# A two-layer convolution kernel: the first statistics read from row sums, two reductions for the kernel's sum, and other orders later

## The chip, the cores and the metric

The kernel runs on one core of a Trainium2 chip. The metric is the time of one execution on the device in microseconds, as the median of several runs. The engines are TensorE (PE in the profile, PEld its weight loads), VectorE (DVE), ScalarE (ACT), GpSimd (POOL) and SyncE (SP, which issues the DMAs). Each executes its own queue in order; semaphores tie them together.

## The reference

```python
# x: (16, 32, 48, 48) float32; L0 weight: (32, 32, 3), L0 bias: (32,); L1 weight: (32, 32, 5, 5)
def _L0_conv_ref(x, weight, bias):          # 9 x 9 Gaussian kernels made of (sx, sy, angle)
    w = _gaussian_kernels(weight, 9)        # exp(-q / 2), divided by its sum over the 81 taps
    out = conv(x, w, padding=4)
    return out + bias[None, :, None, None]
def _L1_conv_ref(x, weight):                # 5 x 5 convolution with reflected edges
...
def _gn(v, G=16, eps=1e-05):                # normalise each image's 16 groups of two channels
    g = v.reshape(B, G, C // G, H, W)
    return ((g - mean(g)) / sqrt(var(g) + eps)).reshape(v.shape)
x = x + _L0_conv_ref(_gn(x), L0_conv_weight, L0_conv_bias)
x = x + _L1_conv_ref(_gn(x), L1_conv_weight)
```

## The kernel before

The 16 images lie as 8 pairs in the on-chip array X, with channel and row modulo 4 on the 128 partitions. Two pairs are a quad (`qd`, four images), so layer 1 runs in four quads; layer 2 runs by pairs. Both convolutions are done along the rows with a short-filter transform: layer 1 makes 8 streams of 384 columns out of the normalised rows (`s32_1`), each is split into a 16-bit high half (`hi`, a copy by ScalarE) and a low half (`lo`, a subtraction by VectorE), and TensorE multiplies high by high, low by high and high by low weights (`whl`), nine taps each, 27 products per stream (`conv1`, `layer1`). The products of the streams are combined by ScalarE (`read_m1`: `mb`) and VectorE (`middle1`: `ps`, `pd`; `rows1`, `end1`) and added to X. Layer 2 does the same with four streams (`streams2`, `conv2`, `middle2`, `rows2`, `end2`).

There is no scheduler: each engine's order is written out by hand, VectorE's in `first_quad` to `last_steps`, ScalarE's and TensorE's at the end of their blocks. A helper's first argument is the layer or the quad. `low_halves(1, 2, range(2))` makes the first two low halves of layer 1's quad 2; `channel_sums(c, qd, images)` sums images and their squares on ScalarE, two passes for each image; `stats(c, qd)` is the product on TensorE that adds those sums over a group; `small_stats` turns them into scale (`gsc`) and offset (`gof`) on VectorE, with ScalarE's square root (`std`) in the middle.

The first quad is special, since the weights are made while it begins. VectorE makes the exponents of the Gaussian taps (`arg`), ScalarE the exponentials in two parts (3 taps, then 2), VectorE adds the blocks for stream 1 (`outer_blocks`, `all_blocks`, each in two parts), sums the kernel's taps (`tap_pairs`, `kernel_sum`) and multiplies by the reciprocal. Taps beyond the centre are made once and turned: through TensorE for streams 1 and 2 (`turn_partitions`, `turned_kernel`), by DMA for the rest (`turn_kernel`). `FIRST_PARTS` is TensorE's order of made and turned parts. Streams 1 and 2 of quad 0 don't wait for normalised images: TensorE sums raw rows (`near_rows`), and scale and offset are applied to the sums (`first_stream1`, `first_stream2`), so stream 1 needs X, the scale and the offset. The images' mean comes from `plain`: twelve products of X with the group matrix, 192 columns each, summed once more by `first_means` on VectorE. `warming` keeps TensorE at work until X lands.

## Time and profile before

| | |
|---|---|
| median of 3 runs | 241.84 us (240.73, 241.84, 244.12) |
| profiled execution | 240.74 us, span 238.9 us |
| busy: TensorE, VectorE, ScalarE | 97%, 89%, 66% of the span |
| the chain that ended last | PE 52%, DVE 34%, ACT 6%, issue 5% |

The span is from the first to the last instruction of the profiled execution; 1.8 us of its time lie around it. A matmul in 32-bit floats appears as two records. The chain is followed back from the last instruction, at each step to what released it; from 110.9 us on it is TensorE alone, before that mostly VectorE.

### The profile page before, as it was taken

The numbers are of one execution on the slowest core, as the hardware profiler recorded it, in microseconds if no ns is written. First come the engines' busy times: TensorE is split into PE (matmuls) and PEld (weight loads), VectorE is DVE, ScalarE is ACT, GpSimd is POOL, SyncE is SP. The second block draws the span as 40 slices with busy tenths as digits, with TensorE's granted clock in tenths as the row PEclk, the third lists the DMA queues.
The fourth block names the chain that finished last, engine by engine and source line by source line (L and its number), as shares of the span: only waits on it lengthen the run. The fifth ranks groups of instructions, "written<-read, shape, count | busy, mean of one in ns | idle before, by whom it ended". The sixth has DMA issues, their size and how long they took to land.

```text
span 238.9 us, 4161 instructions
## 1 busy us (share of the span) xinstructions
PE 231.8 (97%) x1445; PEld 144.2 (60%) x1445; DVE 211.5 (89%) x460; ACT 157.9 (66%) x329; POOL 4.5 (2%) x12
## 2 busy tenths in 40 slices
PE   6999999899999999999999999999999999999995
PEld 6855656555665665555666665556666665555554
DVE  5999999899999899999989998999997459978943
ACT  6979899897598487999637693537459004569310
POOL 1000000320000000000000000000000000000000
PEclk9999999999999999999999999999999999999999
DMA  7980122210034000003502000162020002521123
GB/s 211 377 344 4 36 54 68 67 44 0 3 103 112 3 1 0 3 0 105 186 26 99 0 4 0 35 171 111 1 101 0 0 0 59 155 102 60 44 99 99
DMA packets 8709, 17.24 MB, mean 72 GB/s; under 512 B 3312, under 2 KB 5616, under 8 KB 8688
## 3 DMA queue, kind: packets, MB, share of 16 engines
q1 hardware_dynamic: 7712, 16.64, 21.2%
q10 hardware_dynamic: 976, 0.34, 0.6%
q8 instruction: 11, 0.18, 0.3%
q14 instruction: 10, 0.08, 0.1%
HBM read 5.57 MB, written 4.72 MB: 43 GB/s over the span
## 4 chain that ended last, share of the span: by engine, by line
PE 52%; DVE 34%; ACT 6%; issue 5%; DMA 1%; DVEq 0%; ACTq 0%
PE banks L1477 28%; PE banks L1494 25%; DVE X L796 7%; DVE lo L763 4%; DVE whl L565 2%; ACT junk L1098 2%; DVE wl L590 1%; ACT hi L1154 1%; DVE work L560 1%; ACT P L1131 1%; DMA prm<-in_w 1%; DVE partU L712 1%; ACT arg L1178 1%; DVE s L496 1%; DVE partU L677 1%
## 5 line engine op out<-in xcount | busy, mean ns | idle before, releaser
L1477 PE MATMUL banks<-hi,whl 128*128 128x360 f16 (+4 forms) x576 | 98.2, 318 | 1.0 <-DVE pd L787 0.7
L1477 PEld LDWEIGHTS banks<-hi,whl 128*128 128x128 f16 x576 | 55.5, 98 | 35.4 <-DVE pd L787 1.0
L1477 PE MATMUL banks<-lo,whl 128*128 128x376 f16 (+4 forms) x288 | 51.2, 318 | 1.0 <-DVE lo L763 1.0
L1098 ACT ACTIVATE junk<-X 128x576 bf16<-128x576 f32 x56 | 41.1, 734 | 2.1 <-DVE X L796 0.5
L1477 PEld LDWEIGHTS banks<-lo,whl 128*128 128x128 f16 x288 | 27.8, 97 | 18.3 <-DVE lo L763 1.7
L1494 PE MATMUL banks<-lo,wh 128*128 128x384 f16 (+1 forms) x165 | 31.5, 320 | 0.0
L1494 PE MATMUL banks<-hi,wl 128*128 128x384 f16 (+1 forms) x165 | 31.5, 320 | 0.0
L1494 PE MATMUL banks<-hi,wh 128*128 128x384 f16 (+1 forms) x165 | 31.5, 320 | 0.0
L1154 ACT CAST hi<-work 128x416 f16<-128x416 f32 x32 | 16.6, 537 | 17.7 <-PE banks L1494 12.6
L1144 ACT ACTIVATE work<-work,gof,gsc 128x26 f32<-128x26 f32 (+1 forms) x48 | 24.9, 609 | 3.6 <-DVE gof L661 3.6
L1154 ACT CAST hi<-s 128x384 f16<-128x384 f32 x32 | 15.3, 510 | 16.6 <-DVE s L730 11.0
L1494 PEld LDWEIGHTS banks<-hi,wl 128*128 128x128 f16 x165 | 15.7, 96 | 10.5
L1494 PEld LDWEIGHTS banks<-lo,wh 128*128 128x128 f16 x165 | 15.7, 96 | 10.5
L1494 PEld LDWEIGHTS banks<-hi,wh 128*128 128x128 f16 x165 | 15.8, 96 | 10.4
L763 DVE TENSOR_TENSOR lo<-work,hi 128x416 f16<-128x416 f32 x32 | 17.4, 583 | 1.0 <-ACT hi L1154 0.8
L796 DVE SCALAR_TENSOR_TENSOR X<-pd,X 128x384 f32<-128x384 f32 x36 | 18.1, 558 | 0.0
L796 DVE SCALAR_TENSOR_TENSOR X<-ps,X 128x384 f32<-128x384 f32 x36 | 18.1, 558 | 0.0
L1131 ACT ACTIVATE P<-X,gof,gsc 128x336 f32<-128x336 f32 x28 | 17.2, 687 | 0.5 <-DVE gof L661 0.5
L763 DVE TENSOR_TENSOR lo<-s,hi 128x384 f16<-128x384 f32 x32 | 16.4, 552 | 0.6 <-ACT hi L1154 0.2
L786 DVE SCALAR_TENSOR_TENSOR ps<-banks,mb 128x384 f32<-128x384 f32 x12 | 6.6, 554 | 8.0 <-PE banks L1477 7.2
L1165 ACT ACTIVATE mb<-banks,bias 128x384 f32<-128x384 f32 x12 | 6.8, 568 | 7.7 <-PE banks L1477 7.7
L1098 ACT ACTIVATION_READ_ACCUMULATOR junk<-X 128x1 f32 x56 | 10.6, 190 | 0.0
(137 smaller groups left out, 232.0 us busy)
## 6 DMA issues: line engine op xcount, KB each, us to landing
X<-in_x SPq DMA_DIRECT2D x8, 576.0 KB, 9.4
out<-X SPq DMA_DIRECT2D x7, 576.0 KB, 2.8
work<-X SPq DMA_DIRECT2D x8, 432.0 KB, 3.8
whl<-work SPq DMA_DIRECT2D x24, 64.0 KB, 2.0
work<-X SPq DMA_DIRECT2D x8, 144.0 KB, 3.6
stage<-in_w SPq DMA_DIRECT2D x1, 640.0 KB, 7.3
work<-X SPq DMA_DIRECT2D x32, 12.0 KB, 2.3
out<-X SPq DMA_DIRECT2D x1, 384.0 KB, 2.6
```

Of the source, the lines that this page charges most:

```text
L496: done(tt(ca[:, at, :].rearrange("p k (e o) -> p k e o", o=C), centre.unsqueeze(1).to_broadcast([P, n, NE, C]), ak[:, at, :].unsqueeze(2). ...
L565: tt(made_taps(wl, i), weight1(i), made_taps(wh, i), ALU.subtract).then_inc(wl1_done, 1)
L763: tt(lo[c][:, i, :], src, hi[c][:, i, :], ALU.subtract).then_inc(lo_done[c], 1)
L786: stt(ps[1][:, :], product1(qd, k), f, mb[1][:, :], ALU.mult, ALU.add).then_inc(mid_done[1], 1)
L796: stt(out1(qd, k), tiled1(src[1][:, :]), factors[g][i], out1(qd, k), ALU.mult, ALU.add).then_inc(out_done[1], 1)
L1098: nc.scalar.activation(waste, image(n, m), function, accum_out=sums[c][:, col:col + 1]).then_inc(sums_done[c], 1)
L1131: ins = nc.scalar.activation(dst, src, ACT.Identity, bias=gof[1][:, i:i + 1], scale=gsc[1][:, i:i + 1])
L1144: ins = nc.scalar.activation(dst[:, :, d0:d1_:ds_], src[:, :, s0:s1:ss], ACT.Identity, bias=gof[2][:, i:i + 1], scale=gsc[2][:, i:i + 1])
L1154: nc.scalar.copy(hi[c][:, i, :], src).then_inc(hi_done[c], 1)
L1165: nc.scalar.activation(mb[1][:, :], src, ACT.Identity, bias=bias_c[1 if g == 0 else 2][:, 0:1], scale=FIRST1[g]).then_inc(m_read[1], 1)
L1477: ins = nc.tensor.matmul(dst[:, :, y0:y1], w[1][:, i, t * P:(t + 1) * P], src[:, :, y0 + IMG * dx:y1 + IMG * dx], start=(first and part == ...
L1494: ins = nc.tensor.matmul(dst, wbuf[2][:, i, j * P:(j + 1) * P], src[:, rows, IMG * t:IMG * t + ROW], start=(part == 0 and t == 0), stop=(p ...
```

## The change

`plain` and its twelve products are gone. Stream 1's near rows are summed by halves (`near_half`, six products of 192 columns a half), with two more a half into a second bank: the inner rows times 5.25. Near sum plus inner sum is the plain sum of all rows, so `first_row_sums` reduces both banks on VectorE, and one small product (`first_sums`) makes the mean. Stream 2's near rows follow around it. The kernel's sum comes from one reduction over the centre tap and one over all five made taps. The table is copied in one part, two factors are made ahead of the exponentials' table load, stream 1's weights are scaled and copied in two parts, three warming products are added. Later, the second quad's statistics are split around a low half, `read_m1(0, 0)` comes ahead of two sums, ScalarE's first two high halves of quad 1 are put between its sums, `stats(2, 0)` is asked for inside a stream, and two low halves come ahead of `rows2(0)`.

```diff
-WARMING = 8
-
-PLAIN_BANK, PLAIN_ROWS = 3, 2
-
-
-
-NEAR_FACTORS = (-4.25, -1.0, 4.25)
+WARMING = 11
+
+INNER_BANK = 5
+
+INNER_FACTOR = 3
+
+
+
+NEAR_FACTORS = (-4.25, -1.0, 4.25, 5.25)
 NEAR_OFFSET = 2.0 * (1.0 + 1.0 - 4.25)
-NEAR_BANK = {1: 4, 2: 5}
+NEAR_BANK = {1: 4, 2: 3}
...
-            def tap_pairs():
+            def kernel_centre():
                 dve.wait_ge(dve_w, MARK["all blocks"])
-                done(tt(by_two, slot(1)[:, 0:2, :], slot(1)[:, 2:4, :], ALU.add))
+                done(nc.vector.tensor_reduce(centre_sum, slot(1)[:, PAD1, :].rearrange("p (r o) -> p o r", o=C), AX_X, ALU.add))
+
+            def kernel_taps():
+                dve.wait_ge(dve_w, MARK["all blocks"])
+                done(nc.vector.tensor_reduce(sum_all, slot(1).rearrange("p k (r o) -> p o k r", o=C), AX_XY, ALU.add))
+                MARK["taps"] = count[0]
             def kernel_sum():
-
-                stage_end()
-                done(tt(by_one, by_two[:, 0, :], by_two[:, 1, :], ALU.add))
-                stage_end()
-                done(stt(by_all, by_one, 2.0, slot(1)[:, PAD1, :], ALU.mult, ALU.add))
-                stage_end()
-                done(nc.vector.tensor_reduce(ksum[:, :], by_all.rearrange("p (r o) -> p o r", o=C), AX_X, ALU.add))
+                dve.wait_ge(dve_w, MARK["taps"])
+                done(stt(ksum[:, :], sum_all, 2.0, centre_sum, ALU.mult, ALU.subtract))
...
+            def first_row_sums():
+                dve.wait_ge(near_mm, 1)
+                dve.wait_ge(inner_mm, 1)
+                both = banks[:, NEAR_BANK[1]:INNER_BANK + 1, 0:OUTN].rearrange("p b (n y m) -> p n m b y", n=2, m=IMG)
+                for n in range(2):
+                    ins = nc.vector.tensor_reduce(sums[1][:, n * IMG:(n + 1) * IMG], both[:, n, :, :, :], AX_XY, ALU.add)
+                ins.then_inc(rows_summed, 1)
+
             def first_means():
-                dve.wait_ge(plain_mm, IMG)
-                sums_of = banks[:, PLAIN_BANK, 0:QI * PLAIN_ROWS * W].rearrange("p (n y m) -> p n m y", n=2, m=IMG)
-                step(nc.vector.tensor_reduce(first_mean.rearrange("p (n m) -> p n m", m=IMG), sums_of, AX_X, ALU.add))
+                dve.wait_ge(stat_mm, 2)
+                step(nc.vector.tensor_copy(first_mean, STAT[1][:, 0:QI]))
...
-            def small_stats(c, n):
+            def stats_variance(c, n):
...
+            def stats_scales(c, n):
+
+                mean = mom[c][:, 0, :]
+                at = SMALL * n
                 dve.wait_ge(std_done[c], n + 1)
...
+                outer_blocks(0)
+                all_blocks(0)
+                first_row_sums()
+                kernel_centre()
+                outer_blocks(1)
                 first_means()
-                outer_blocks(0)
+                all_blocks(1)
                 first_variance()
-                all_blocks(0)
-                outer_blocks(1)
+                kernel_taps()
                 first_root()
-                all_blocks(1)
+                kernel_sum()
                 first_newton()
-                tap_pairs()
+                kernel_reciprocal()
                 first_scales()
-                kernel_sum()
-                kernel_reciprocal()
                 dve.wait_ge(dve_w, MARK["krec"])
-                flat1 = slot(1).rearrange("p k (r o) -> p (k r) o", o=C)
-                done(stt(flat1, flat1, W_SCALE, krec[:, :].unsqueeze(1).to_broadcast([P, NT * RB, C]), ALU.mult, ALU.mult))
-                MARK["weights", 1] = count[0]
+                for step_at, taps in enumerate(STEPS2):
+                    at = slice(*taps)
+                    flat1 = slot(1)[:, at, :].rearrange("p k (r o) -> p (k r) o", o=C)
+                    done(stt(flat1, flat1, W_SCALE, krec[:, :].unsqueeze(1).to_broadcast([P, (taps[1] - taps[0]) * RB, C]), ALU.mult, ALU.mult))
+                    MARK["weights", 1, step_at] = count[0]
...
-                small_stats(1, 1)
+                stats_variance(1, 1)
                 low_half(1, 0, 7)
+                stats_scales(1, 1)
                 low_kernel(6)
...
+                low_halves(1, 2, range(2))
                 rows2(0)
-                low_halves(1, 2, range(2))
...
-            act.dma_start(tab[:, 0:TAB], tables[:, 0:TAB]).then_inc(tab_loaded, 16)
-            act.dma_start(tab[:, TAB:], tables[:, TAB:]).then_inc(identity_loaded, 16)
+            act.dma_start(tab[:, :], tables).then_inc(tab_loaded, 16)
...
+            near_factors((0, INNER_FACTOR))
             nc.scalar.activation(warm[:, :], bias_c[2][:, :], ACT.Exp)
-            channel_sums(1, 0, range(2))
-            near_factors((0,))
-            channel_sums(1, 0, range(2, 4))
+            channel_sums(1, 0)
             kernel_exponentials()
...
+            read_m1(0, 0)
             channel_sums(1, 1, range(3, 4))
-            read_m1(0, 0)
...
-            channel_sums(1, 2, range(2))
-            high_halves(1, 1, range(2))
+            channel_sums(1, 2, range(1))
+            high_halves(1, 1, range(1))
+            channel_sums(1, 2, range(1, 2))
+            high_halves(1, 1, range(1, 2))
...
+            def near_half(n):
                 pe.wait_ge(x_loaded[n], 16)
-                part = PLAIN_ROWS * ROW
-                dst = banks[:, PLAIN_BANK, n * part:(n + 1) * part]
-                steps = T // PLAIN_ROWS
-                for k in range(steps):
-                    src = pair(n)[:, k * part:(k + 1) * part]
-                    ins = nc.tensor.matmul(dst, group_t, src, start=(k == 0), stop=(k == steps - 1))
-                ins.then_inc(plain_mm, 1)
-
-            def near_rows(i, steps):
-
-                terms = (((0, identity_t), (4, identity_t), (1, identity_t), (5, identity_t), (2, factors1[:, 0, :]), (3, factors1[:, 0, :]))
-                         if i == 1 else
-                         ((1, identity_t), (5, identity_t), (0, factors1[:, 1, :]), (4, factors1[:, 1, :]), (2, factors1[:, 2, :]), (3, factors1[:, 0, :])))
-                dst = tiled1(banks[:, NEAR_BANK[i], 0:OUTN])
+                halves = slice(n * TILES1, (n + 1) * TILES1)
+                dst = tiled1(banks[:, NEAR_BANK[1], 0:OUTN])[:, halves, :]
+                inner = tiled1(banks[:, INNER_BANK, 0:OUTN])[:, halves, :]
+                for at, row in enumerate((0, 4, 1, 5)):
+                    nc.tensor.matmul(dst, identity_t, out1(0, row)[:, halves, :], start=(at == 0), stop=False)
+                pe.wait_ge(factors_made, 2)
+                for row in (2, 3):
+                    ins = nc.tensor.matmul(dst, factors1[:, 0, :], out1(0, row)[:, halves, :], start=False, stop=(row == 3))
+                if n == 1:
+                    ins.then_inc(near_mm, 1)
+                for row in (2, 3):
+                    ins = nc.tensor.matmul(inner, factors1[:, INNER_FACTOR, :], out1(0, row)[:, halves, :], start=(row == 2), stop=(row == 3))
+                if n == 1:
+                    ins.then_inc(inner_mm, 1)
...
+            def first_squares():
+                pe.wait_ge(sums_done[1], QI)
+                nc.tensor.matmul(STAT[1][:, QI:], group_t, sums[1][:, QI:], start=True, stop=True).then_inc(stat_mm, 1)
+
+            def first_sums():
+                pe.wait_ge(rows_summed, 1)
+                nc.tensor.matmul(STAT[1][:, 0:QI], group_t, sums[1][:, 0:QI], start=True, stop=True).then_inc(stat_mm, 1)
...
+                        if between is not None:
+                            stats(*between)
...
-            for n in range(2):
-                plain(n)
-            stats(1, 0)
-            pe.wait_ge(identity_loaded, 16)
-            near_rows(1, range(6))
-            near_rows(2, range(6))
+            near_half(0)
+            near_half(1)
+            first_squares()
+            near_rows(range(2))
+            first_sums()
+            near_rows(range(2, 6))
...
-                layer1(1, k)
+                layer1(1, k, between=(2, 0) if k == 5 else None)
                 if k == 3:
                     weight_mean()
-                if k == 4:
-                    stats(2, 0)
```

VectorE's order, from the last exponents on, before (`work` holds the block sums, `L608` is the mean, `L617` the clamped variance, `L621` the reciprocal of the deviation):

```order
L504 SCALAR_TENSOR_TENSOR arg<-s_1 128x384 x4
L608 TENSOR_REDUCE mom<-banks 128x4
L610 SCALAR_TENSOR_TENSOR msq<-mom 128x4
L510 TENSOR_TENSOR work<-arg 128x384
L615 TENSOR_TENSOR var<-banks,msq 128x4
L617 TENSOR_SCALAR vare<-var 128x4
L516 TENSOR_TENSOR work<-work,arg 128x384
L510 TENSOR_TENSOR work<-arg 128x256
L621 RECIPROCAL rcp<-std 128x4
L623 SCALAR_TENSOR_TENSOR msq<-vare,rcp 128x4
```

and after (`L513`, `L519` the block sums, `L613` the row sums, `L618` the mean, `L627` the clamped variance, `L524` and `L528` the sums over centre tap and all taps):

```order
L507 SCALAR_TENSOR_TENSOR arg<-s_1 128x384 x4
L513 TENSOR_TENSOR work<-arg 128x384
L519 TENSOR_TENSOR work<-work,arg 128x384
L613 TENSOR_REDUCE sums<-banks 128x2 x2
L524 TENSOR_REDUCE work<-work 128x32
L513 TENSOR_TENSOR work<-arg 128x256
L618 COPY mom<-banks 128x4
L620 SCALAR_TENSOR_TENSOR msq<-mom 128x4
L519 TENSOR_TENSOR work<-work,arg 128x256
L625 TENSOR_TENSOR var<-banks,msq 128x4
L627 TENSOR_SCALAR vare<-var 128x4
L528 TENSOR_REDUCE work<-work 128x32
```

The mean moved behind two block additions and two reductions, and the long reduction stands between the clamped variance and the reciprocal that follows it.

ScalarE's order between two bias reads of quad 0, before (`junk,sums` the sums of quad 2's images, `hi` quad 1's high halves):

```order
L1165 ACTIVATE mb<-banks,bias 128x384
L1098 ACTIVATE junk,sums<-X 128x576 x4
L1154 CAST hi<-s_1 128x384 x2
L1165 ACTIVATE mb<-banks,bias 128x384
L1098 ACTIVATE junk,sums<-X 128x576 x4
L1154 CAST hi<-s_1 128x384 x2
```

and after:

```order
L1188 ACTIVATE mb<-banks,bias 128x384
L1121 ACTIVATE junk,sums<-X 128x576 x2
L1177 CAST hi<-s_1 128x384
L1121 ACTIVATE junk,sums<-X 128x576 x2
L1177 CAST hi<-s_1 128x384
L1188 ACTIVATE mb<-banks,bias 128x384
L1121 ACTIVATE junk,sums<-X 128x576 x4
L1177 CAST hi<-s_1 128x384 x2
```

The first high half moved ahead of two sums, the second stayed behind four.

VectorE's order behind quad 2's first two streams, before (`lo` their low halves, the three rows of `X<-X` layer 2's updates):

```order
L724 TENSOR_TENSOR s_1<-partU 128x384 x2
L796 SCALAR_TENSOR_TENSOR X<-ps,X 128x4x96 x3
L796 SCALAR_TENSOR_TENSOR X<-pd,X 128x4x96 x3
L815 TENSOR_TENSOR X<-X,ps 128x4x96
L815 TENSOR_TENSOR X<-X,pd 128x4x96
L815 TENSOR_TENSOR X<-X,ps 128x4x96
L763 TENSOR_TENSOR lo<-s_1,hi 128x384 x2
```

and after:

```order
L743 TENSOR_TENSOR s_1<-partU 128x384 x2
L815 SCALAR_TENSOR_TENSOR X<-ps,X 128x4x96 x3
L815 SCALAR_TENSOR_TENSOR X<-pd,X 128x4x96 x3
L782 TENSOR_TENSOR lo<-s_1,hi 128x384 x2
L834 TENSOR_TENSOR X<-X,ps 128x4x96
L834 TENSOR_TENSOR X<-X,pd 128x4x96
L834 TENSOR_TENSOR X<-X,ps 128x4x96
```

The two low halves moved ahead of the three updates.

## Rows read from the trace of the kernel before

**Rows 1.** Two stretches: length, PE, PEld, DVE, ACT, POOL busy, clock, DMA, GB/s

```profile
17.20:111.00 93.80, 91.21 (x576) 55.06 (x575) 89.83 (x185) 79.81 (x166) 3.56 (x2) 1.00 0.13 34
111.00:236.30 125.30, 125.27 (x806) 77.12 (x805) 107.71 (x234) 64.85 (x137) 0.00 (x0) 1.00 0.20 65
```

**Rows 2.** Timeline of TensorE, head: start, length, operation, count, [idle before it <- releaser]

```profile
0.99 3.59 PE L1553 MATMUL banks<-ones 128*128 128x128 f32 x16 [0.99 <-POOL ones L1375]
5.52 4.14 PE L1426 MATMUL banks<-X,tab 128*128 128x192 f32 x24 [0.94 <-DMA X<-in_x]
9.49 0.28 PE L1411 MATMUL banks<-sums,tab 128*128 128x4 f32 x2
9.63 2.83 PE L1441 MATMUL banks<-X,tab 128*128 128x384 f32 x8
12.29 1.45 PE L1441 MATMUL banks<-X,factors 128*128 128x384 f32 x4
```

**Rows 3.** Timeline of ScalarE, head

```profile
9.15 1.90 ACT L1178 ACTIVATE arg<-arg 128x1152 f32<-128x1152 f32 x2
...
12.57 0.49 ACT L1110 ACTIVATE factors<-tab 128x128 f32<-128x128 f32 x2
...
14.30 1.41 ACT L1118 ACTIVATE s<-banks,off,gsc 128x96 f32<-128x96 f32 x4 [1.05 <-DVE gof L635]
...
15.74 0.51 ACT L1154 CAST hi<-s 128x384 f16<-128x384 f32 x1
...
16.42 0.72 ACT L1182 CAST whl<-work 128x640 f16<-128x640 f32 x1 [0.17 <-DVE work L883]
```

**Rows 4.** The exponentials' line: shortest, median and longest duration in ns

```profile
L1178 ACT ACTIVATE arg<-arg x2: 826/994/1162, 9.2 to 10.2; 128x1152 f32<-128x1152 f32 x1, 128x768 f32<-128x768 f32 x1
```

**Rows 5.** Timeline of VectorE, head

```profile
9.97 0.55 DVE L608 TENSOR_REDUCE mom<-banks 128x4 f32<-128x384 f32 x1
...
14.05 0.15 DVE L635 SCALAR_TENSOR_TENSOR gof<-mom,gsc 128x4 f32<-128x4 f32 x1
...
14.77 0.38 DVE L530 TENSOR_REDUCE ksum<-work 128x32 f32<-128x128 f32 x1
...
15.18 0.35 DVE L535 RECIPROCAL krec<-ksum 128x32 f32<-128x32 f32 x1
...
15.56 0.83 DVE L883 SCALAR_TENSOR_TENSOR work<-work,krec 128x640 f32<-128x640 f32 x1
...
16.39 0.55 DVE L763 TENSOR_TENSOR lo<-s,hi 128x384 f16<-128x384 f32 x1
```

**Rows 6.** DMA issues of the first 8 us: KB each, us to landing

```profile
tab<-in_tables ACTq DMA_DIRECT2D x1, 80.0 KB, 2.1
tab<-in_tables ACTq DMA_DIRECT2D x1, 64.0 KB, 4.4
```

**Rows 7.** Timelines of the three engines, 40 to 118 us

```profile
42.24 0.56 DVE L786 SCALAR_TENSOR_TENSOR ps<-banks,mb 128x384 f32<-128x384 f32 x1 [0.76 <-ACT mb L1165]
...
46.24 0.95 PE L1477 MATMUL banks<-lo,whl 128*128 128x384 f16 x5 [0.69 <-DVE lo L763]
...
53.66 0.91 ACT L1154 CAST hi<-s 128x384 f16<-128x384 f32 x2
...
54.19 1.02 DVE L763 TENSOR_TENSOR lo<-s,hi 128x384 f16<-128x384 f32 x2
...
54.31 1.55 PE L1477 MATMUL banks<-hi,whl 128*128 128x384 f16 x9 [0.69 <-DVE pd L787]
...
62.14 0.98 ACT L1154 CAST hi<-s 128x384 f16<-128x384 f32 x2 [3.71 <-DVE s L730]
...
76.44 0.39 PE L1416 MATMUL banks<-sums,tab 128*128 128x8 f32 x2 [0.57 <-ACT junk L1098]
...
110.90 1.57 PE L1477 MATMUL banks<-lo,whl 128*128 128x384 f16 x9 [0.33 <-DVE lo L763]
...
115.54 0.98 ACT L1154 CAST hi<-s 128x384 f16<-128x384 f32 x2 [1.89 <-DVE s L730]
```

More of the change, by code:

```diff
@@ L124, in casts @@
     at = FIRST_ORDER.index(i)
-    return at + 1 + (1 if at >= FIRST_ORDER.index(2) else 0)
+    return at + 1 + sum(at >= FIRST_ORDER.index(j) for j in SPLIT)
 def order1(qd):
@@ L232, in build @@
         WMEAN = banks[:, 7, 4 * QI:4 * QI + 1]
-        READS = ((1, 0), (1, 1), "mean", (2, 0), (1, 2), (1, 3), (2, 1), (2, 2), (2, 3))
+        READS = ((1, 0), "first sums", (1, 1), "mean", (2, 0), (1, 2), (1, 3), (2, 1), (2, 2), (2, 3))
         x_loaded = [sem(f"x_loaded{n}") for n in range(NP)]
@@ L1402, in bank7 @@
                 at = READS.index(key)
-                if at > 0:
-                    pe.wait_ge(first_step_done, 3)
-                wait(pe, stat_read, at - 1)
+                pe.wait_ge(first_step_done, 3)
+                wait(pe, stat_read, at - 2)
             def stats(c, qd):
@@ L1409, in stats @@
                 pe.wait_ge(sums_done[c], summed(c, qd + 1) - (QI if shared else 0))
-                if (c, qd) == (1, 0):
-                    nc.tensor.matmul(STAT[1][:, QI:], group_t, sums[1][:, QI:], start=True, stop=True).then_inc(stat_mm, 1)
-                    return
                 if shared:
@@ L1435, in near_rows @@
                 for step in steps:
-                    if i == 1 and step == 4:
-                        pe.wait_ge(factors_made, 1)
-                    if i == 2 and step == 2:
+                    if step == 2:
                         pe.wait_ge(factors_made, len(NEAR_FACTORS))
@@ L1451, in _, with conv1 @@
             TAPS = (PAD1,) + tuple(t for t in range(K1) if t != PAD1)
-            def conv1(qd, k, taps=TAPS, first=True, last=True):
+            def conv1(qd, k, taps=TAPS, first=True, last=True, between=None):
                 i = S1[k]
@@ L1471, in conv1 @@
                     for t in taps:
-                        if qd == 0 and first and part == 0 and i == 2 and t == STEPS2[1][1] - 1:
+                        if qd == 0 and first and part == 0 and i in SPLIT and t == STEPS2[1][1] - 1:
                             pe.wait_ge(wh1_done, casts(2))
@@ L1506, in _, with layer1 @@
             held = {}
-            def layer1(qd, k):
+            def layer1(qd, k, between=None):
                 bank = BANKS1[qd][k]
@@ L1511, in layer1 @@
                     pe.wait_ge(*held[bank])
-                conv1(qd, k)
+                conv1(qd, k, between=between)
                 held[bank] = READ1[k](qd)
```

32 lines of the change are left out of this document (19 added, 13 removed).

## The prediction

> **What bounds the kernel now.** I read the profile in four steps. First the busy time of each engine in two long stretches [rows 1]: from 111.0 us to 236.3 us TensorE is busy 125.27 of 125.30 us, so nothing there waits and the end is where TensorE's last stretch begins plus a constant. Between 17.2 and 111 us it is busy 91.21 of 93.80 us: 2.6 us are lost in waits. Second, those waits one by one in the timeline [rows 7]: 0.69 us at 46.24, 0.69 us at 54.31, 0.57 us at 76.44 and 0.33 us at 110.90 (the rest is a few tenths). VectorE is busy 89.83 of the same 93.80 us [rows 1], so behind each of TensorE's waits stands a row of VectorE and ScalarE work with hardly a gap. So two things can move the end: the time at which the first convolution starts (the head, up to 17.2 us), since the VectorE row starts with it, and TensorE's waits in the middle. Third, the head on TensorE [rows 2]: warming, then the twelve plain sums (4.14 us), then twelve near products of 384 columns; eight records, two to a product, bring it from 9.63 to 12.29, so one takes 0.665 with the wait for the first factor's load, and I use 0.65. Fourth, the head on ScalarE and VectorE [rows 3, 5]: scale and offset are ready at 14.20, ScalarE makes stream 1 (14.30 to 15.71), its high half (to 16.25) and the high weights (16.42 to 17.14), and TensorE starts at 17.2. TensorE itself ends its near rows at 17.4, so all three engines come out together. Time taken from one of them alone buys nothing, and a later scale costs at once.
>
> **TensorE's head.** Removed: twelve plain products of 192 columns, 4.14 us for 12, so 0.32 us at the spacing of the loads. The near sums of stream 1 (6 products of 384 columns, 3.9 us) become 16 products of 192 columns, 16 x 0.32 = 5.2 us. 8.0 us of work becomes 5.2: TensorE is relieved of 2.8 us. Three more warming products add at most 3 x 3.59 / 8 = 1.3 us behind 4.58, to 5.9 us; X lands at about 5.5, so 0.2 to 0.4 us of it shows. Near and inner sums are then ready at 5.7 + 5.2 = 10.9 us, and all near rows at about 15.8 us in place of 17.4.
>
> **ScalarE's head.** Two factor copies now stand ahead of the exponential's table load; two take 0.49 us [rows 3]. One of them stood between the squares before, where it hid all but 0.05 us, and 0.1 us of waiting for X disappears. The first exponential therefore starts at 9.50 in place of 9.15. This needs the merged table copy to be there at 3.8 us: its first part landed 2.1 us after an issue at 0.74, and 64 KB more should add some tenths [rows 6]. See the rivals for the other case.
>
> **VectorE's head** is the term that decides. I lay the new order out with the durations of the rows [rows 4, 5]. The first exponential (1.16 us) ends at 10.66. Two dependent additions of 384 columns (0.55 each and 0.04 between dependents) end at 11.80. The row sums are two reductions of 384 columns from PSUM; the one of before took 0.55, and a second starts 0.47 behind: 12.8. TensorE's product for the mean needs its loads and two passes, 0.28 us for the passes [rows 2] and, estimated at the plain products' spacing of loads, 0.16 ahead of them: 0.44: 13.25. Behind it stand in this order: copy, square, the addition of 256 columns, variance, clamp, at 0.2 us for each small dependent step (0.15 of work, as in the offset's row, and 0.04 behind it) and 0.35 for the addition: 14.3 us. Before, the mean came from one reduction at 9.97. Now comes the long reduction over 640 columns. It is not in the trace. Its bounds are 0.83 (the scaling pass of 640 columns) and 0.94 (0.38 for the reduction of 128 columns into the same 32 sums, and 512 columns more at 0.28 us for 256, the step from 0.55 to 0.83); I take 0.9, nearer to its own kind. It stands ahead of the reciprocal of the deviation, which ScalarE has had since 14.5: 15.1. Then reciprocal, square, kernel sum, Newton step, kernel reciprocal (0.35), scale and the two offsets: 16.25. **The offset is ready 2.05 us later than before (14.20).** What this bought, the kernel's reciprocal, is not earlier either: 15.9 in place of 15.53.
>
> Why so late, when TensorE gave up 2.8 us? The row sums wait behind two additions which wait for the exponential, so TensorE's relief (sums ready at 10.9) meets a VectorE that comes for them only at 11.7; and the reduction of 0.47 us left VectorE while two of them and the 0.9 us came.
>
> **From there to the convolution.** ScalarE: 16.3 + 1.41 + 0.51 = 18.2. VectorE's first low half starts at 18.3 in place of 16.39: +1.9 us, and it idles from 17.1. The split weights help here: the first part, 384 columns, costs as much as the high half, 0.51 us at 0.1 overlap, and TensorE starts at 18.7 in place of 17.2; the undivided copy would be 0.2 us later. But the low weights and all of VectorE's row are 1.9 later, so the advance is lost within one stream. Head: **+1.9 us** (bounds: 1.3 if the exponential is not pushed and the long reduction takes 0.83 with the small steps packed closer; 2.4 if each new wait costs 0.05 more and the exponential starts at 9.6).
>
> A rule of the Trainium skill can be held against this: VectorE: DVE Perf Modes, Rules for kernel authors, calls the reduction the slowest VectorE operation and advises against it on a hot path. The rows show a reduction of 384 columns at the 0.55 us of an addition of 384 columns [rows 5]; by the page one might price the long pass higher, by the rows it is its place in the queue that costs, not its rate.
>
> **The orders later.** (a) The bias read of stream 1 moves ahead of two sums on ScalarE: VectorE's 0.76 us gap at 42.24 closes. With the variance split around a low half, VectorE is about 0.4 us early at 46.8, and the low half is ready before TensorE asks, so the 0.69 us at 46.24 goes. But VectorE then waits for the normalised image, which ScalarE makes at the same time as before, and TensorE, 0.69 us early, only comes so much earlier to the waits that (b) treats, whose ends are set by VectorE. I count 0 for (a) by itself. (b) ScalarE now makes the first high half of quad 1 between two pairs of sums, 0.9 us earlier: the 0.69 us at 54.31 goes, which is put down to VectorE's pd but ends when the high half of 53.66 does. The second high half, however, comes behind two more sums, at 54.75 to 55.26; VectorE's second low half started at 54.67 (0.47 behind the first) and now starts at 55.30, with everything behind it. That is **+0.63 us** on VectorE's row, and TensorE's third stream of the quad starts just when ScalarE's high half of 62.14 ends (62.65), so TensorE is 0.63 us later there too and nothing of the 0.69 remains. (c) The sums of layer 2 are asked for after the first third of a stream, 1.4 us later: **-0.57 us** (the wait at 76.44). (d) The low halves stand ahead of three row updates of VectorE (3 x 0.47 = 1.4 us): **-0.33 us** (the wait at 110.90), with 1.1 us to spare for VectorE's delay. From then on TensorE is 0.9 us nearer to VectorE; the third stream's high half of the next quad is ready at 116.05 [rows 7], where TensorE, at 4.2 us a stream from 109.0, asks for it at about 118, so I expect no new wait.
>
> **Sum.** 1.9 + 0.63 - 0.57 - 0.33 = +1.6 us. The profiled execution takes 240.74 us for a span of 238.9; +1.6 makes 242.3. The median of the runs is 241.84, 1.1 above the profiled one; on it the sum is 243.4. I do not know which part of those 1.1 us the change would touch (some of it may be TensorE's head, which is shorter now), and take 242.6, nearer to the profiled base. A measurement of this kernel can tell about 2% from no change, 4.8 us.
>
> **Rivals.** *The orders later give back more than the head costs.* If the delay of 0.63 us does not come through, and the waits of 46.24 and 54.31 go for good, then 1.9 - 0.69 - 0.69 - 0.57 - 0.33 = -0.4: 240.3 to 241.4. For it: these four waits are all that TensorE loses. Against: the third stream's start at ScalarE's high half, a tenth of a microsecond of TensorE's time. Chance 0.2.
>
> *The head is no later.* If the waits on ScalarE and between small steps overlap more than I lay out, so that the offset is ready at 14.7 and the convolution starts at 17.2: 0.0 + 0.63 - 0.9, 240.5 on the profiled base. Against: ten dependent steps stand in the order, and none of them can be skipped. Chance 0.12.
>
> *Slower: the table lands late.* The table was copied in two parts; the second landed 4.4 us after its issue, between X's packets [rows 6]. If the merged copy lands like that, at 5.6 us, then VectorE's step of 4.83 waits 0.8 us, and ScalarE's factors wait from 3.8 to 5.6, and with them table load, squares and exponential: 1.8 us more on the chain to the mean. 242.3 + 1.8 = 244.1 to 245. It decides from a landing after 4.8 us. For it: the copy is larger and stands ahead of X. Against: it is issued 0.45 us ahead of X, and the first part was in well before X's. Chance 0.1.
>
> *Slower: TensorE's clock falls before the first convolution.* The warming products of 128 columns are spaced 0.43 us, the 192-column ones behind them 0.32: the first are at 1.2 GHz, the later at 2.4, though the granted clock reads 1.00 in both [rows 1, 2]. TensorE now idles 2.9 us (15.8 to 18.7), where before its longest idle stretch was 0.94 us and no fall followed. If it restarts at the lower level and stays there as long as at the start (3.6 us), it does half the work in that time: +1.8 us, 244.1. The Trainium skill says so too: TensorE: Matmul & The Clock Gate, HAM oscillation, an engine kept waiting falls back to half rate. By that rule it would be 244.1; no row shows a fall. Chance 0.1.
>
> **How the numbers follow.** My forecast, +1.1 to +2.3 us, has 0.48. The range 240.6 to 244.6 takes in the forecast on both bases, most of the second rival and half of the first, and the late table and the clock at their price. Faster by over 2% needs -4.8 us, more than all waits of TensorE: 0.03. Slower by over 2% needs both slow rivals and more, or a new wait in every quad: 0.06. Within 2%: 0.91.
>
> **What would show it.** In the profile after: the first exponential at 9.5 us; the row sums at 11.7; the offset at 16.2; VectorE idle for 1.1 us ahead of its first low half; the first convolution at 18.7. A gap of about 0.6 us on VectorE ahead of the second low half of quad 1; no wait of TensorE for sums in quad 1 and none at the start of quad 2. If the convolution starts at 17.2 or earlier, my layout of VectorE's head is wrong. If the third stream of quad 1 does not wait, (b) is wrong. If TensorE waits again past 112 us, the slack I read there was not enough.

## The result, and the profile after

The changed kernel takes 247.43 us (median of four executions, 245.58 to 248.41), the kernel before 241.31 in the same comparison (240.73 to 244.12): a ratio of 1.023, 95% interval 1.018 to 1.027. Slower by 6 us where 0.8 were forecast, and outside the forecast's range. The profiled execution takes 245.58 us for a span of 243.8, 4.8 more than the profiled one of before.

TensorE's waits in the profile after (line, what it waited for: us in total, times, longest):

```profile
PE banks L1510 <- ACT whl L1211: 3.0, 1, 3.0
PE banks L1464 <- ACT factors L1133: 1.8, 1, 1.8
PE banks L1510 <- ACT hi L1177: 1.3, 1, 1.3
```

The first two are new and in the head, and the prediction's sum has neither. The third is the third stream of quad 1, as term (b) said. The waits for low halves, for `pd` and for the sums of [rows 7] are gone. One of 0.4 us for turned weights (`DMA whl<-work`) is new with the later orders; every run that has them shows it, e5 and e10 too. The largest wait is for `whl`, the high weights. Timeline of TensorE and ScalarE after, 15.5 to 28.5 us, answering to [rows 2, 3]:

```profile
15.50 4.36 PE L1464 MATMUL banks<-X,factors 128*128 128x384 f32 x8 [1.81 <-ACT factors L1133]
...
18.97 0.81 ACT L1211 CAST whl<-work 128x384 f16<-128x384 f32 x2
...
19.70 0.64 PE L1510 MATMUL banks<-hi,whl 128*128 128x384 f16 x3
...
22.42 0.82 ACT L1211 CAST whl<-work 128x384 f16<-128x384 f32 x2
...
23.29 0.48 PE L1510 MATMUL banks<-hi,whl 128*128 128x360 f16 x2 [2.95 <-ACT whl L1211]
...
25.63 1.07 ACT L1230 CAST whl<-banks 128x512 f16<-128x512 f32 x2 [1.22 <-PE banks L1565]
...
28.40 0.58 ACT L1230 CAST whl<-banks 128x512 f16<-128x512 f32 x1 [1.07 <-PE banks L1565]
```

ScalarE copied both parts of stream 1's weights between 18.97 and 19.78. TensorE does three products and stops, and goes on at 23.29, just after ScalarE's *next* pair of copies (22.42 to 23.24), which are stream 2's. The code says why. `casts(i)` is the number of weight copies done once stream i's are complete; with stream 1 in two parts it is 2 for stream 1 and 4 for stream 2. The wait ahead of the fourth product, which before stood for stream 2 alone, now serves both and asks for `casts(2)`. Stream 1 waits for four copies where two are its own.

This would be TensorE's loss alone if TensorE had no customers. But it also turns stream 1's weights for ScalarE (`L1565`), ScalarE waits 1.22 and 1.07 us for them, and behind that stands the third stream's high half. VectorE after, head, answering to [rows 5]:

```profile
12.23 1.01 DVE L613 TENSOR_REDUCE sums<-banks 128x2 f32<-128x384 f32 x2
...
14.64 0.17 DVE L627 TENSOR_SCALAR vare<-var 128x4 f32<-128x4 f32 x1
14.71 1.23 DVE L528 TENSOR_REDUCE work<-work 128x32 f32<-128x640 f32 x1
...
16.86 0.15 DVE L645 SCALAR_TENSOR_TENSOR gof<-mom,gsc 128x4 f32<-128x4 f32 x1
...
19.09 0.56 DVE L782 TENSOR_TENSOR lo<-s,hi 128x384 f16<-128x384 f32 x1 [1.18 <-ACT hi L1177]
...
29.43 0.56 DVE L782 TENSOR_TENSOR lo<-s,hi 128x384 f16<-128x384 f32 x1 [2.30 <-ACT hi L1177]
```

The offset is ready at 17.01 (16.25 forecast, 14.20 before), the first low half starts at 19.09 (18.3; 16.39), and the third waits 2.30 us. VectorE's row, the one that sets the end, has taken over TensorE's stall. VectorE's second and third low half before, and the second after:

```profile
20.40 0.55 DVE L763 TENSOR_TENSOR lo<-s,hi 128x384 f16<-128x384 f32 x1
...
24.52 0.56 DVE L763 TENSOR_TENSOR lo<-s,hi 128x384 f16<-128x384 f32 x1
```

```profile
23.11 0.55 DVE L782 TENSOR_TENSOR lo<-s,hi 128x384 f16<-128x384 f32 x1
```

They are 4.12 us apart before and 6.32 after (the third is the one at 29.43). So the first low half is 2.70 us later than before and the third 4.91, and the span is 4.9 longer: what the two profiled executions differ by is all there by 30 us.

The windows of one microsecond show something else (length, PE, PEld, DVE, ACT, POOL busy, granted clock, DMA share, GB/s):

```profile
15.00:16.00 1.00, 0.50 (x1) 0.50 (x2) 1.00 (x2) 0.63 (x4) 0.00 (x0) 0.59 1.05 424
16.00:17.00 1.00, 1.00 (x3) 0.40 (x2) 0.92 (x9) 0.00 (x0) 0.00 (x0) 0.50 0.68 272
17.00:18.00 1.00, 1.00 (x3) 0.62 (x2) 0.91 (x4) 0.89 (x3) 0.00 (x0) 0.50 0.10 41
18.00:19.00 1.00, 1.00 (x3) 0.53 (x2) 0.00 (x0) 0.97 (x4) 0.00 (x0) 0.71 0.00 0
19.00:20.00 1.00, 1.00 (x5) 0.48 (x4) 0.91 (x2) 1.00 (x4) 0.00 (x0) 1.00 0.00 0
```

After 1.8 us of idle TensorE restarts at the lower level (1.2 GHz), and its eight records of 384 columns take 4.36 us. This is the fall that the fourth rival spoke of, one idle stretch earlier than I had placed it; what it costs is seen below (e9). The Trainium skill (TensorE: Matmul & The Clock Gate, HAM oscillation) has an engine that waits long enough between its products fall back to half rate; the trace agrees here, while e1 shows the same wait without a fall.

### The profile page after: what moved, and what is told of

Same layout as the page of the kernel before. It is cut to its first block, busy times and chain, and to the rows that moved or that the text cites. A ratio compares the mean times of both kernels' runs of the same rounds, so it can differ in the third digit from the quotient of the medians.

```text
span 243.8 us, 4174 instructions
## 1 busy us (share of the span) xinstructions
PE 232.5 (95%) x1449; PEld 145.3 (60%) x1449; DVE 212.3 (87%) x462; ACT 158.1 (65%) x331; POOL 4.5 (2%) x12
## 3 DMA queue, kind: packets, MB, share of 16 engines
HBM read 5.57 MB, written 4.72 MB: 42 GB/s over the span
## 4 chain that ended last, share of the span: by engine, by line
DVE 43%; PE 30%; ACT 12%; issue 9%; DMA 3%; DVEq 0%; SPq 0%; ACTq 0%
PE banks L1527 16%; PE banks L1510 14%; DVE X L815 9%; DVE lo L782 5%; ACT junk L1121 4%; ACT P L1154 3%; DMA X<-in_x 3%; ACT hi L1177 2%; DVE wl L593 1%; DVE X L834 1%; DVE whl L568 1%; DVE ps L805 1%; DVE partU L731 1%; DVE partU L696 1%; DVE partB L734 1%
```

## The experiments

Most executions of the kernel before lie in one of two clusters of times (about 240.9 and 242.5 us; the last section has what the traces show of them), so small differences are read between lowest times as well as medians. VectorE's row sets the end, so its low halves give a second measure, read in one trace: the start of the first tells what the head ahead of it costs, and the distance between the second and the third, which the clusters do not touch, what the late count costs.

**e1: the count.** The changed kernel with one expression altered.

```diff
                         if qd == 0 and first and part == 0 and i in SPLIT and t == STEPS2[1][1] - 1:
-                            pe.wait_ge(wh1_done, casts(2))
+                            pe.wait_ge(wh1_done, casts(i))
```

> The changed kernel with one value changed: ahead of the fourth product of stream 1, TensorE waits for stream 1's own second weight copy (the third of the copies' count) and no longer for the count at which stream 2's second copy is made too. Theory A (the wrong count): TensorE's wait of 2.95 us between its third product at 19.7 us and its fourth at 23.3 us goes, the turned kernels come earlier, ScalarE's wait for them (1.22 and 1.07 us) shrinks, and VectorE's third low half, 4.9 us later than in the kernel before, is only 2.7 us later: 2.2 us less than the changed kernel, about 243.4 us in a profiled run. Theory B (the late offset and the lower clock of TensorE from 15 to 18.5 us make the whole loss): less than 0.5 us is won, since ScalarE and VectorE are late anyway.

Measured: 243.2 us (243.02 to 243.95), 1.0064 [1.0037, 1.009] of before: 4.2 us less than the changed kernel, by one number. Part of it is no effect of the number alone, since three of the changed kernel's four executions also show a lower clock (e9). Timeline of e1, the same stretch:

```profile
14.46 1.24 DVE L528 TENSOR_REDUCE work<-work 128x32 f32<-128x640 f32 x1
...
15.25 2.85 PE L1464 MATMUL banks<-X,factors 128*128 128x384 f32 x8 [1.81 <-ACT factors L1133]
...
18.85 0.56 DVE L782 TENSOR_TENSOR lo<-s,hi 128x384 f16<-128x384 f32 x1 [1.18 <-ACT hi L1177]
...
19.28 0.95 PE L1510 MATMUL banks<-hi,whl 128*128 128x384 f16 x5 [1.19 <-ACT whl L1211]
...
22.86 0.55 DVE L782 TENSOR_TENSOR lo<-s,hi 128x384 f16<-128x384 f32 x1
...
26.99 0.56 DVE L782 TENSOR_TENSOR lo<-s,hi 128x384 f16<-128x384 f32 x1
```

All five products stand in one group now, and 4.13 us lie between the second and third low half, as before; the late count cost 2.2. The first low half starts 2.46 us later than before, and the span is 2.5 longer (241.4 against 238.9). What is left of the loss is the head.

**e2: the factors too.** e1, with stream 2's two factors made ahead of the square root.

```diff
+            near_factors((1, 2))
             nc.scalar.activation(warm[:, :], bias_c[2][:, :], ACT.Sqrt)
             standard_deviation(1, 0)
-            near_factors((1, 2))
```

> As e1_wait_fixed, and the two factor copies for stream 2's near rows stand ahead of the square root on ScalarE, so that TensorE need not wait from 13.7 to 15.5 us for them. Theory A1 (that idle stretch is what made the clock fall): the granted clock stays at 1.00 up to the first convolution or falls later, the near rows end at 16.5 in place of 19.6 us; the time moves little against e1_wait_fixed, 0 to 0.5 us less, because the offset and not the near rows sets the start. Rival A2: the idle stretch only moves to 16.5 to 19.5 us, the clock falls inside it, and the first convolutions run at the lower level: 0.5 to 1.5 us slower than e1_wait_fixed.

Measured: 243.78 us (243.55 to 244.09), 1.0100 [1.0069, 1.0131]: 0.6 us slower than e1. The idle stretch did not go, it moved. Windows of two microseconds of e2:

```profile
14.00:16.00 2.00, 1.92 (x6) 0.77 (x5) 1.86 (x9) 0.39 (x2) 0.00 (x0) 1.00 1.02 415
16.00:18.00 2.00, 0.00 (x0) 0.00 (x0) 1.43 (x7) 1.33 (x4) 0.00 (x0) 1.00 0.42 168
18.00:20.00 2.00, 0.92 (x4) 0.51 (x5) 1.35 (x3) 1.97 (x6) 0.00 (x0) 0.84 0.00 0
20.00:22.00 2.00, 2.00 (x8) 1.01 (x7) 2.00 (x6) 2.00 (x5) 0.00 (x0) 0.50 0.02 4
```

Before the convolution TensorE now stands still for 3.16 us, and it is the convolution, with customers, that runs at half rate. VectorE's second and third low half stand at 22.66 and 27.38, 4.72 us apart where e1 has 4.13: 0.6 us lost. (Of the seven executions one has a mean clock of 1.00, and it is no faster: 244.09 us.) A wait in front of work that nobody waits for was the better place.

**e3 and e4: the split alone.** The kernel before with stream 1's weights scaled and copied in two parts (the scaling stands in the diff ahead); e3 with the late count, e4 with its own.

```diff
-            high_kernel(1)
+            high_kernel_parts(1)
...
-                        if qd == 0 and first and part == 0 and i == 2 and t == STEPS2[1][1] - 1:
+                        if qd == 0 and first and part == 0 and i in SPLIT and t == STEPS2[1][1] - 1:
                             pe.wait_ge(wh1_done, casts(2))       # e3; casts(i) in e4
```

> The kernel before, with the split of stream 1's weights alone, and with the changed kernel's count in the wait (stream 2's copies). Theory A: the count costs by itself 2.2 to 2.6 us against the kernel before, since TensorE does twelve products of stream 1 and the first turn only after 20.3 us, when stream 2's copy is there, and ScalarE and VectorE wait for the turned kernels. Theory B: under 0.5 us slower.

> The kernel before, with the split of stream 1's weights alone and the right count. All theories: the first convolution starts up to 0.2 us earlier, but TensorE ends its near rows at 17.4 us and waits for stream 2's weights at 20.3 us anyway: 0 to 0.2 us from the kernel before, either way.

Measured: e3 244.56 us (244.23 to 245.11), 1.0128 [1.0082, 1.0174]; e4 242.23 (240.91 to 242.62), 1.0011 [0.9981, 1.0042]. By medians the late count costs 2.3 us on a head that is otherwise the old one, where the profile has TensorE waiting 1.9 us (`ACT whl L1191` in the list of waits). The two spans differ by 3.3 us (242.4 and 239.1), but they come from different clusters: the plain sums take 5.95 us in e3's trace and 4.14 in e4's, and e3's first low half is 1.1 us later for it. VectorE's second and third low half, first of e3, then of e4:

```profile
21.67 0.55 DVE L764 TENSOR_TENSOR lo<-s,hi 128x384 f16<-128x384 f32 x1
...
28.02 0.56 DVE L764 TENSOR_TENSOR lo<-s,hi 128x384 f16<-128x384 f32 x1 [2.33 <-ACT hi L1157]
```

```profile
20.54 0.55 DVE L764 TENSOR_TENSOR lo<-s,hi 128x384 f16<-128x384 f32 x1
...
24.68 0.56 DVE L764 TENSOR_TENSOR lo<-s,hi 128x384 f16<-128x384 f32 x1
```

They are 6.35 us apart with the late count and 4.14 without: 2.2 us, the same as on the changed kernel. The split itself costs and gives nothing that these runs can show.

**e5 and e6: the later orders alone.** The kernel before with all of them (e5), and without term (b) (e6); the lines of (b):

```diff
-            channel_sums(1, 2, range(2))          # e5 only
-            high_halves(1, 1, range(2))
+            channel_sums(1, 2, range(1))
+            high_halves(1, 1, range(1))
+            channel_sums(1, 2, range(1, 2))
+            high_halves(1, 1, range(1, 2))
```

> The kernel before with all four later orders of the change and nothing else of it. The prediction's terms: +0.63 for the second high half behind two more sums, -0.57 for the sums asked for inside a stream, -0.33 for the low halves ahead of three updates: -0.3 us in a profiled run against the kernel before. Rival (all four waits of TensorE go for good): -2.2 us. Read beside it: VectorE's gap ahead of the second low half of quad 1 (0.6 us), and whether TensorE waits for the third stream's high half.

> As e5_orders, but ScalarE makes the first two high halves of quad 1 together behind the sums, as in the kernel before. By the prediction's terms the 0.63 us disappear and the other two stay: -0.9 us against the kernel before, faster than e5_orders by 0.6 us. Rival: the wait of 0.69 us at the start of quad 1, which only that order removes, matters more: slower than e5_orders by up to 0.7 us.

Measured: e5 241.94 us (240.47 to 242.59), 1.0002 [0.9968, 1.0036]; e6 241.44 (240.05 to 241.98), 0.9980 [0.9947, 1.0012]. By lowest times against before's 240.79 in that comparison: -0.3 and -0.7. e5's second low half of quad 1, and e6's first two in one row:

```profile
56.82 0.56 DVE L771 TENSOR_TENSOR lo<-s,hi 128x384 f16<-128x384 f32 x1 [0.69 <-ACT hi L1163]
```

```profile
54.34 1.03 DVE L771 TENSOR_TENSOR lo<-s,hi 128x384 f16<-128x384 f32 x2 [0.17 <-ACT hi L1163]
```

With (b) VectorE waits 0.69 us ahead of the second low half; without it the two follow each other. Between e5 and e6 lie 0.4 us by lowest times and 0.5 by medians. In the traces it is 0.7: the spans differ by 2.0 us, and 1.3 of these are the later first low half of e5, whose plain sums ran slowly (last section).

**e7: the head alone.** e1 with all later orders put back.

```diff
-                stats_variance(1, 1)
+                small_stats(1, 1)
                 low_half(1, 0, 7)
-                stats_scales(1, 1)
...
-                low_halves(1, 2, range(2))
                 rows2(0)
+                low_halves(1, 2, range(2))
...
```

> The changed kernel with the right count (e1_wait_fixed) and the kernel before's later orders: the new head by itself. VectorE's first low half came 2.46 us later there than in the kernel before, so +2.5 us in a profiled run, 243.2, if the orders' sum is small as predicted (then it equals e1_wait_fixed to 0.3 us). If the orders gave back 2 us there, this one is at 245.

Measured: 243.35 us (243.1 to 243.51), 1.0089 [1.0055, 1.0122], against e1's 243.2 in another comparison. Its span is 0.3 us longer than e1's (241.7 and 241.4), and its first low half is 0.3 later (19.18 and 18.85), so behind the head the orders give nothing here. The head costs 2.5 to 2.8 us.

**e8: the old pair sums.** e1 with the kernel's sum as before, by pairs and behind the scale.

```diff
-                done(nc.vector.tensor_reduce(sum_all, slot(1).rearrange("p k (r o) -> p o k r", o=C), AX_XY, ALU.add))
+                done(tt(by_two, slot(1)[:, 0:2, :], slot(1)[:, 2:4, :], ALU.add))
...
-                kernel_centre()
...
-                kernel_taps()
+                tap_pairs()
                 first_root()
-                kernel_sum()
                 first_newton()
-                kernel_reciprocal()
                 first_scales()
+                kernel_sum()
+                kernel_reciprocal()
```

> The changed kernel with the right count (e1_wait_fixed) and the kernel's sum made the old way: one addition of pairs of taps (256 columns), and the rest of the sum behind the scale and the offsets; no reduction over 640 columns, which took 1.24 us there, and none over the centre tap. If those two reductions and their place ahead of the scale are what makes the head late, the offset is ready at 15.2 in place of 16.77 us, the first convolution starts near 17.9 in place of 19.3, and the time falls 1.4 us, to 241.8. Rival (the row sums' place behind the exponentials is the cause): at most 0.5 us less.

Measured: 242.3 us (241.98 to 243.0), 1.0021 [0.9994, 1.0048], 0.9 less than e1. Timeline of e8:

```profile
8.66 0.75 ACT L1120 ACTIVATE junk<-X 128x576 bf16<-128x576 f32 x1 [1.00 <-DMA X<-in_x]
...
10.33 1.89 ACT L1200 ACTIVATE arg<-arg 128x1152 f32<-128x1152 f32 x2
...
15.81 4.44 PE L1463 MATMUL banks<-X,factors 128*128 128x384 f32 x8 [1.77 <-ACT factors L1132]
...
16.34 0.15 DVE L645 SCALAR_TENSOR_TENSOR gof<-mom,gsc 128x4 f32<-128x4 f32 x1
```

Though the exponentials start 0.6 us later than in e1 (X's second pair came later), the offset starts 0.28 earlier (16.34 against 16.62). So the two reductions stand for 0.9 us of the scale's delay. From the exponentials to the offset 1.1 us are left over before; the order puts them down to the row sums behind the block additions, but no run takes those alone. The first low half gains less than the offset, 0.1 us (18.75 against 18.85), since the kernel's sum now stands ahead of it.

**e9: TensorE kept at work.** The changed kernel, late count and all, with unread products on the warming bank in its two idle stretches: 8 behind the sums' product, 13 ahead of the fourth product. Their results are used by nothing.

```diff
                         if qd == 0 and first and part == 0 and i in SPLIT and t == STEPS2[1][1] - 1:
+                            if i == 1:
+                                warming(13)
                             pe.wait_ge(wh1_done, casts(2))
...
             first_sums()
+            warming(8)
             near_rows(range(2, 6))
```

> The changed kernel with its late count, and products that nobody reads put into TensorE's two idle stretches: 8 of the warming kind ahead of the near rows that wait for their factors, 13 ahead of stream 1's fourth product (the output is as before). Theory C (part of the loss is TensorE's clock, which falls in those stretches: 0.986 on average in the slower executions): the mean granted clock is 1.00 and the median falls from 247.4 to 245.5, to what the late count (2.4 us) and the head (2.5 us) explain without the clock. Rival (the clock costs nothing, since TensorE is ahead anyway): 247.4 to within 0.3, or more by what the products themselves take.

Measured: 245.97 us (245.58 to 246.19), 1.0197 [1.0162, 1.0231], mean granted clock 0.999 to 1.00 in all four executions. The changed kernel's four: 245.58 at a mean clock of 0.993, then 248.06, 246.8 and 248.41 at 0.985 to 0.986. The filler takes nothing for itself: TensorE still waits 0.24 us for `whl` behind the thirteen products, and VectorE's second and third low half are 6.36 us apart, as in the changed kernel (6.32).

So the fall ahead of the near rows costs nothing in the traced execution of the changed kernel. Its time is 245.58 us, the lowest of e9 too. e7 and e8 have the same fall and their usual 4.1 us between the low halves, and e1's five executions at a mean clock of 0.993 lie within 0.2 us of its four at 1.00 by medians. What the filler takes away are the three longer executions: 1.5 us by the medians, 0.7 by the ratios. The traced fall lowers the mean by 0.007 and the longer executions are 0.014 to 0.015 below 1, so they were at the lower level for about twice as long (an estimate from these means). Where, no trace shows; the idle from 20.3 to 23.3, with the convolution behind it as in e2, is my guess.

**e10 and e11: what is worth keeping.** The kernel before with eleven warming products (e11), and with the later orders less (b) as well (e10).

```diff
-WARMING = 8
+WARMING = 11
```

> The kernel before with the three good later orders (e6_orders_less_one) and 11 warming products in place of 8, the plain sums kept. In the executions of the kernel before with a late end (242.1 to 243.0, about half of them) the plain sums run at the lower level: 5.86 us for twelve in one such trace, where others take 4.14. If the longer warming lifts the clock ahead of X in every execution, the median falls to 240.1, 0.5 to 0.9% under the kernel before. Rival (X's landing and not the warming decides, or the three more products delay the sums): 241.4, as e6_orders_less_one, with the same spread.

> The kernel before with 11 warming products and nothing else. If the clock is what spreads its executions: median 240.9 with a spread under 0.5 us. Rival: 241.9, spread from 240.8 to 243.

Measured: e11 240.99 us (240.8 to 241.31), 0.9964 [0.9938, 0.999]; e10 240.09 (239.98 to 240.22), 0.9926 [0.9902, 0.995]. e10 is faster than both kernels: 2.3 us under before's median in that comparison (242.35), 0.6 under its lowest time (240.71). Between e10 and e11, with no clusters left to blur it, the orders (a), (c) and (d) together are worth 0.90 us, which is what the prediction has for (c) and (d) (0.57 and 0.33) with nothing for (a).

**e12: the table in one copy.** The kernel before with that part of the change alone.

```diff
-            act.dma_start(tab[:, 0:TAB], tables[:, 0:TAB]).then_inc(tab_loaded, 16)
-            act.dma_start(tab[:, TAB:], tables[:, TAB:]).then_inc(identity_loaded, 16)
+            act.dma_start(tab[:, :], tables).then_inc(tab_loaded, 16)
```

> The kernel before with the table copied by one DMA and nothing else. In the changed kernel the second pair of X landed at 8.3 us, where squares wait 0.68 us, and the parameters at 3.0 in place of 2.7. If the merged copy does that: +0.3 to +0.6 us (VectorE's first step 0.3 later, the third square at 8.0 or later). Rival (X's landing varies from run to run by itself): 0 +- 0.2 us.

Measured: 241.69 us (241.12 to 242.95), 1.0005 [0.9975, 1.0035]; its lowest is 0.4 above before's lowest (240.71). TensorE in e12, the two halves of the plain sums, [rows 2] of before:

```profile
6.06 2.19 PE L1424 MATMUL banks<-X,tab 128*128 128x192 f32 x12 [1.29 <-DMA X<-in_x]
8.50 2.22 PE L1424 MATMUL banks<-X,tab 128*128 128x192 f32 x12 [0.25 <-DMA X<-in_x]
```

The table was there in time, but X came later. For the first pair (6.06 where it was 5.52) the table need not be the cause, since e5, with the table in two copies, has 5.98. For the second pair the traces point to it. In the seven traces with two copies the third square waits 0.23 us at most and the exponentials start at 9.15 to 9.43; in the seven with one copy they start at 9.53 to 10.33, and in six of these the square waits 0.37 to 1.00 us for X. e12, where nothing else is changed, has 10.15, and its first low half is 1.0 us later than before. (In the others the forecast itself put 0.35 us of delay down to the early factor copies.) That is one trace; the times of e12 show 0.4 us by lowest values and nothing clear of noise by medians. As far as this goes, the factors that the change needs early are paid for by X.

## Why the prediction was wrong

**The step that failed** is "The split weights help here ... and TensorE starts at 18.7". I priced the split as a copy made shorter, 0.2 us in its favour, and took for granted that each part is waited for by its own count. The count it waits for belongs to stream 2. TensorE started at 19.70, stopped after three products for 2.95 us, and passed the stop on to VectorE. The sum had no such term. The runs show it at 2.2 us on VectorE's row, on the changed kernel (against e1) and on the old head (e3 against e4); by medians it is 2.3 on the old head and 4.2 on the changed kernel, clock included.

**The clock rival** had 0.1, and came true in half. The fall is there (idle, then 1.2 GHz), but I looked for the idle in one place. I counted the near rows of stream 2 as following each other to 15.8, though four of the six products need factors that ScalarE makes behind the square root; before, those were there at 13.1 [rows 3] and asked for at 14.9. They waited 1.8 us, the clock fell there, and that fall costs nothing, since only stream 2 reads these rows. The rival priced the idle ahead of the convolution, at 1.8 us. e2 has that idle (3.16 us) and the convolution at half rate behind it, and loses 0.6. In the changed kernel the lower clock costs 0.7 to 1.5 us (against e9), in executions that no trace shows.

**The head** was to cost 1.9, 2.4 at most, and costs 2.5 to 2.8 (first low halves and spans of e1 and e7 against before's; 2.7 in the changed kernel). It was mis-sized in two terms. The long reduction takes 1.23 us where I took 0.9 with 0.94 as the upper bound. My second bound added columns at the price of an elementwise pass. The Trainium skill (VectorE: DVE Perf Modes, Rules for kernel authors), which calls the reduction VectorE's slowest operation, was nearer than my rows: 640 columns cost 1.23 as a reduction, 0.83 as a scaling pass. The other is X. The third square waits 0.68 us for its pair and the exponentials start at 9.98, not 9.50; e12 has that with the table in one copy alone. I had asked only whether the table lands in time, not what lands behind it. The rest of the layout held: 0.48 and 0.33 make up the 0.76 us by which the offset is later than forecast, and VectorE's idle ahead of its first low half is 1.18 for 1.1.

**The later orders** were right term by term on the old head. (b) gives VectorE a gap of 0.69 to 0.70 us in e5, e1 and the kernel after, for 0.63, and TensorE a wait of 1.31 for the third stream's high half. (a), (c) and (d) give 0.90 together (e10 against e11). All four: -0.3 by lowest times, -0.27 forecast. On the new head the traces of e1 and e7 show no gain from them; no run shows why. The rival in which the orders give back more than the head costs is refuted, as are the one with a head no later and the late table: ScalarE made its factors from the table at 3.98.

**How the loss divides.** Between the two profiled executions lie 4.9 us of span: 2.7 ahead of VectorE's first low half, which is the new head, and 2.2 between its second and third, which is the late count. The orders add about nothing. The median of the changed kernel is another 1.85 us above its profiled execution; that part goes with the lower mean clock, and 1.5 of it is gone with the filler. e9's median is 2.8 above e1's, more than the 2.2 of the late count, since X came late in e9 and its first low half is 0.5 us later than e1's (19.33 and 18.85).

Where did the 2.8 us of relief for TensorE go? Into idle time. TensorE was no bottleneck in the head, as the prediction said, and what paid for it (row sums, a long reduction, an earlier table) lay on the chain to the scale.

## What to carry to other kernels

Where a change makes a step that signals once signal twice, look up every wait that names the semaphore and write down the count beside the signals that it stands for: a count that is too high shows only as a stall, here of 3 us on the engine that waits and 2.2 us at the end. In the profile such a stall is known by its releaser: the wait ends not with the copy that it needs but with the next one on the same line. And work taken from an engine with slack is worth its idle time only; put what replaces it on the chain's clock first.

## What the runs showed of the hardware

**The level of TensorE's clock in the first microseconds differs from execution to execution, and the column of granted clock doesn't show it.** Timeline of TensorE in e5, whose clock reads 1.00 throughout, and in e10:

```profile
0.99 3.78 PE L1566 MATMUL banks<-ones 128*128 128x128 f32 x16 [0.99 <-POOL ones L1386]
5.98 5.86 PE L1437 MATMUL banks<-X,tab 128*128 128x192 f32 x24 [1.21 <-DMA X<-in_x]
```

```profile
0.99 4.85 PE L1564 MATMUL banks<-ones 128*128 128x128 f32 x22 [0.99 <-POOL ones L1384]
5.82 4.14 PE L1435 MATMUL banks<-X,tab 128*128 128x192 f32 x24
```

The same 24 records take 5.86 or 4.14 us. Behind eight warming products TensorE idles 0.8 to 1.3 us until X lands, and the plain sums may run at either rate: they took 5.95 us behind 0.82 us of idle (e3) and 4.14 behind 1.30 (e4), so the length of this stretch doesn't decide it. The 1.7 us are about the distance of before's two clusters. Behind eleven products there is no idle stretch in e10 and e11, and the eleven executions of e10 lie within 0.24 us, the ten of e11 within 0.51. No trace shows the head of a long execution of before itself; that they are of this kind is inferred from e3 and e5 and from e11's narrow spread.

**The same idle stretch doesn't always lower the clock.** 1.8 us of waiting for the factors were followed by 4.36 us for eight records in the changed kernel, 4.44 in e8 and 4.11 in e7, but by 2.85 in e1.
